# Four of eight normalised tiles of y move from ScalarE to GpSimd in four more batches

## The reference

```python
x = L0_attn_x                                            # (8, 1024, 128)
x = _layernorm(x + _L0_attn_ref(x, wq, wk, wv, wo), axis=-1)
x = _layernorm(x + _L0_ffn_ref(x, w1, b1, w2, b2), axis=-1)

# _layernorm: (x - mean) / sqrt(var + 1e-5), no gain, no bias
# attention: q, k, v = x @ w; rope(q), rope(k); causal softmax(q k^T / 128) @ v @ wo
# ffn: gelu(x @ (alpha1 * sign(w1)).T + b1) @ (alpha2 * sign(w2)).T + b2
```

## Time and profile before

| | |
|---|---|
| median of 3 runs | 279.47 us (278.9 to 280.8) |
| the profiled execution, its own time | 278.4 us |
| its span, first to last instruction | 276.6 us |
| PE busy | 260.7 us, 94% of the span |
| DVE busy | 230.6 us, 83% |
| ACT busy | 224.7 us, 81% |
| POOL busy | 167.2 us, 60% |
| mean granted clock of PE | 0.983 |

### The profile page before, as it was taken

The page is one execution under the profiler, slowest core; times in us unless marked ns, Lnnn a source line. Parts: engine busy times, 40 slices in busy tenths (PEclk is TensorE's granted clock), DMA queues, the critical chain, the costliest instruction groups (busy, mean ns, idle before and its releaser), DMA issues.

```text
span 276.6 us, 5169 instructions
## 1 busy us (share of the span) xinstructions
PE 260.7 (94%) x1478; PEld 209.2 (76%) x1479; DVE 230.6 (83%) x638; ACT 224.7 (81%) x398; POOL 167.2 (60%) x258
## 2 busy tenths in 40 slices
PE   7799999999999999999999999999999999999960
PEld 3588889987688688868879688767885878897630
DVE  2889999999999996999989985999689738537884
ACT  3468964565897989996998999699999699999972
POOL 3033132613625598299912998477829987887772
PEclk9979999999999999999999999999999999999995
DMA  7943486479648936823675309724830720200323
GB/s 180 161 65 71 102 149 108 115 165 192 105 119 186 193 88 153 176 37 85 184 178 122 84 26 246 185 60 126 204 89 5 210 62 0 78 0 2 105 92 110
DMA packets 58012, 31.94 MB, mean 115 GB/s; under 512 B 33408, under 2 KB 54400, under 8 KB 57984
## 3 DMA queue, kind: packets, MB, share of 16 engines
q1 hardware_dynamic: 57024, 30.76, 49.6%
q10 hardware_dynamic: 960, 0.85, 1.2%
HBM read 9.18 MB, written 4.19 MB: 48 GB/s over the span
## 4 chain that ended last, share of the span: by engine, by line
PE 76%; DVE 8%; ACT 5%; DMA 5%; issue 4%; ACTq 1%; POOL 0%; SPq 0%; POOLq 0%; DVEq 0%
PE pair L589 17%; PE bank L606 17%; PE bank L632 5%; PE bank L674 5%; PE bank L620 4%; PE pair L650 4%; PE pair L651 4%; PE bank L682 3%; PE bank L683 3%; DMA out_dram<-res 2%; DMA sin_sb<-in_sin_dram 2%; PE bank L719 2%; PE pair L663 2%; PE bank L639 2%; PE pair L665 2%
## 5 line engine op out<-in xcount | busy, mean ns | idle before, releaser
L391 POOL TENSOR_TENSOR hid_lo<-hid,hid_hi 128x1024 fp32r<-128x1024 f32 x28 | 66.1, 2386 | 21.1 <-ACT hid_hi L1073 21.1
L1002 ACT ACTIVATE prob<-pair,negmax 128x128 f32<-128x128 f32 (+3 forms) x64 | 47.3, 742 | 17.0 <-DVE negmax L1455 15.4
L606 PE MATMUL bank<-probT,xa 128*128 128x512 f32 (+3 forms) x160 | 54.2, 482 | 0.3 <-DVE res L1565 0.3
L1455 DVE CUSTOM_DVE_ANT_0 pair<-pair,mask_row 128x128 f32<-128x128 f32 (+3 forms) x64 | 47.8, 760 | 6.7 <-PE pair L589 6.3
L606 PEld LDWEIGHTS bank<-probT,xa 128*128 128x128 f32 x160 | 29.1, 190 | 20.4 <-issue 15.8
L341 POOL TENSOR_TENSOR xT_lo<-xT,xT_hi 128x512 fp32r<-128x512 f32 x14 | 18.0, 1285 | 40.8 <-ACT xT_hi L1032 40.8
L1465 DVE STREAM_TRANSPOSE turned<-prob 128x128 f32<-128x128 f32 (+7 forms) x56 | 39.5, 723 | 0.5 <-ACT prob L1002 0.5
L589 PE MATMUL pair<-qkT_hi 128*128 128x512 f32 (+3 forms) x96 | 36.5, 380 | 1.4 <-ACT prob L1002 0.6
L589 PE MATMUL pair<-qkT_hi,qkT_lo 128*128 128x512 f32 (+3 forms) x96 | 33.1, 345 | 0.0
L589 PE MATMUL pair<-qkT_lo,qkT_hi 128*128 128x512 f32 (+3 forms) x96 | 33.1, 345 | 0.0
L1066 ACT ACTIVATE hid<-pair,b_sb,alpha 128x1024 f32<-128x1024 f32 x28 | 32.9, 1208 | 0.1
(11 more groups left out here) (116 smaller groups left out, 649.6 us busy)
## 6 DMA issues: line engine op xcount, KB each, us to landing
probT<-turned SPq DMA_DIRECT2D x96, 116.0 KB, 2.3
probT<-turned SPq DMA_DIRECT2D x128, 52.0 KB, 2.0
xq<-in_L_attn_x_dram SPq DMA_DIRECT2D x28, 128.0 KB, 3.9
xa<-in_L_attn_x_dram SPq DMA_DIRECT2D x7, 512.0 KB, 5.1
out_dram<-res SPq DMA_DIRECT2D x7, 512.0 KB, 3.4
hid<-in_L_ffn_w_dram SPq DMA_DIRECT2D x2, 256.0 KB, 3.1
out_dram<-res SPq DMA_DIRECT2D x2, 256.0 KB, 2.3
xa<-in_L_attn_x_dram SPq DMA_DIRECT2D x1, 256.0 KB, 3.6
```

The source lines that it names most:

```text
L391: pool.tensor_tensor(hid_lo[:, j, :], hid[:, j, :], hid_hi[:, j, :].bitcast(F32), ALU.subtract).then_inc(s_hid_lo[j], 1)
L606: ins = pe.matmul(bank_of["px", g, c][:, 0:n * P], xa[c % 2][:, j, :], probT[g][:, :, TG * j:TG * j + n, :].rearrange("p n m i -> p m n i" ...
L1002: act.activation(prob[r % 3][:, 0:(r + 1) * P], pair_of["score", r, c][:, slice(*columns(r))], ACT.Exp, scale=-1.0, bias=negmax[:, r:r + 1 ...
L1455: dve.tensor_tensor_reduce(mine, mine, mask_row[:, T - (r + 1) * P:T], -1.0, -MASKED, ALU.add, ALU.min, negmax[:, r:r + 1]).then_inc(s_max ...
```

## The change

Four calls `second_norm(4, c)` to `second_norm(7, c)` are taken from ACT's list for c = 1, 2, 3 and 4, and written in POOL's list right behind `second_factors(c)`. `SHARED` becomes batches 1 to 6. With it ACT raises `s_y` behind tile 3 in these batches, and `store(c)` also waits for POOL. The lists of PE, DVE and SP stay as they are. Sixteen instructions change engines; none is added or removed. The last hunk of the diff is ACT's list in batch 3; in batches 1, 2 and 4 the four calls stood apart in it and go in the same way. POOL's first call of a group waits for the last factor (`s_ln2`), which POOL itself wrote.

```diff
-    SHARED = (LAST - 2, LAST - 1)
+    SHARED = tuple(range(1, LAST))
...
             second_factors(1)
+            second_norm(4, 1)
+            second_norm(5, 1)
+            second_norm(6, 1)
+            second_norm(7, 1)
             first_factors(1, B - 4)
...
             second_factors(2)
+            second_norm(4, 2)
...
             first_factors(0, B - 3)
...
             second_factors(3)
+            second_norm(4, 3)
...
             first_factors(0, B - 2)
             first_factors(1, B - 2)
             hidden_low(0, B - 3)
...
             second_factors(B - 4)
+            second_norm(4, B - 4)
...
             first_rstd(0, B - 1)
...
             row_copy(7, B - 1)
-            second_norm(4, 3)
-            second_norm(5, 3)
-            second_norm(6, 3)
-            second_norm(7, 3)
             gelu(0, B - 2)
```

More of the change, by code:

```diff
@@ L449, in _ @@
             second_factors(2)
+            second_norm(4, 2)
+            second_norm(5, 2)
+            second_norm(6, 2)
+            second_norm(7, 2)
             first_factors(0, B - 3)
@@ L457, in _ @@
             second_factors(3)
+            second_norm(4, 3)
+            second_norm(5, 3)
+            second_norm(6, 3)
+            second_norm(7, 3)
             first_factors(0, B - 2)
@@ L464, in _ @@
             second_factors(B - 4)
+            second_norm(4, B - 4)
+            second_norm(5, B - 4)
+            second_norm(6, B - 4)
+            second_norm(7, B - 4)
             first_rstd(0, B - 1)
@@ L1306, in _ @@
             second_norm(3, 1)
-            second_norm(4, 1)
             exponentials(5, B - 2)
-            second_norm(5, 1)
-            second_norm(6, 1)
             exponentials(6, B - 2)
-            second_norm(7, 1)
             exponentials(7, B - 2)
@@ L1333, in _ @@
             hidden_high(0, B - 4)
-            second_norm(4, 2)
-            second_norm(5, 2)
             hidden_high(1, B - 4)
@@ L1338, in _ @@
             exponentials(2, B - 1)
-            second_norm(6, 2)
             exponentials(3, B - 1)
@@ L1342, in _ @@
             hidden_high(3, B - 4)
-            second_norm(7, 2)
             exponentials(5, B - 1)
@@ L1390, in _ @@
             second_norm(3, B - 4)
-            second_norm(4, B - 4)
-            second_norm(5, B - 4)
             gelu_half(0, 0, B - 1)
-            second_norm(6, B - 4)
             gelu_half(0, 1, B - 1)
@@ L1397, in _ @@
             gelu_half(0, 3, B - 1)
-            second_norm(7, B - 4)
             y_half(0, B - 2)
```

## The result

| | before | changed |
|---|---|---|
| median of 4 runs | 279.19 us (278.42 to 280.8) | 289.69 us (288.88 to 291.82) |
| ratio | | 1.041, 95% interval 1.035 to 1.048 |
| profiled execution, span | 276.6 us | 287.7 us |
| PE busy | 260.7 us | 263.8 us |
| DVE busy | 230.6 us | 243.9 us |

Slower was forecast, with 5.5 us. It is 10.5 us in the medians and 11.1 us in the two profiled spans. The time lies above the forecast's range, which ended at 286.5 us.

The account below looks back on a forecast made before the run. PE was taken to bound the kernel. Terms -0.1 (ACT), 0 (batch 2), 4.2 (batch 3), 1.2 (clock) and 0.2 (batch 4) gave +5.5 us on 278.4, so 283.9, forecast as 284.4 us; own range 282 to 286.5, 8-in-10 range from 278.9.

Parts of the forecast that it names:

- relief of ACT is worth 0.1 us: Sixteen norms leaving ACT free 6.7 us there, but gain only 0.1 us, at most 0.6, since PE is busy.
- the list of signs: What the profile would show on each engine; for ACT, busy down by 8 us and waits for DVE and PE up.
- A shift of 1.87 us a group: On POOL, each group of four norms delays what stands behind it by 1.87 us, until POOL's next wait.
- Batch 2 costs nothing, though `first_norm(4, 5)` waits: Near 195 us, first_norm(4, 5) waits some 0.9 us for POOL's later factors; taken as 0, could be 0.4 us.
- Batch 3: norm 0 held by `hidden_low(0, 5)`, norms 4 and 5 one behind each following one, 6 and 7 free: DVE's eight first_norm(t, 6), near 228 us, meet POOL's later hidden_low; up(0, 6) on PE starts 4.2 us late.
- the clock: PE's clock falls to the lower level after its stand near 232 us: 1.2 us, between 0 and 1.7.
- DVE keeps the port: Rival, 19%: after norm 3 of batch 6, norms 4 to 7 follow without a gap while POOL waits; 279.5 us median.
- norms 5 to 7 go together: Rival, 12%: in batch 6 these norms all go ahead of hidden_low(2, 5); +2.1 us, 280.5 to 281.5 us.
- That costs 0.2 us, between 0 and 1.5: Batch 4's group delays first_rstd(0, 7), so first_norm(·, 7) meets hidden_low(0, 6); turn_x1(0, 7) stands behind 52 PE matmuls.

Follow-up runs that it names:

- batches 1 and 2 alone: Only the four-norm groups of batches 1 and 2 moved to POOL, against the kernel before: 279.6 us, ratio 1.001.
- the kernels that have this hole alone: Kernel before with only batch 3's group moved to POOL (283.9 us, 1.016), or with four extra norms on POOL behind second_factors(3) (283.9 us, 1.018).
- batch 4 alone: Only batch 4's four norms moved to POOL, against the kernel before: 285.5 us, ratio 1.023.
- the kernel with batch 4's factor first: Only batch 4's group moved to POOL, with first_rstd(0, 7) ahead of its four norms, against the kernel before: 277.5 us, ratio 0.997.
- batch 3's kernel: Only batch 3's four norms moved to POOL, against the kernel before: 283.9 us, ratio 1.016.
- load on POOL alone: Kernel before plus four POOL norms on a table no longer read, behind second_factors(3); ACT and stores unchanged: 283.9 us, ratio 1.018.

## Why the prediction was right and wrong

- *PE bounds it, relief of ACT is worth 0.1 us.* Right as far as the runs tell: 0, give or take 1.2 us, by the run that leaves the norms out. ACT's busy time fell by 5.2 us; the working had 6.7 and the list of signs 8, both too much.
- *A shift of 1.87 us a group.* Right: from L363's end at 219.43 to L323 at 221.28 it is 1.85, where L323 had started 0.04 us before that end.
- *Batch 2 costs nothing, though `first_norm(4, 5)` waits.* Right: the wait in the profile is 0.8 us, and the run with batches 1 and 2 alone is level.
- *Batch 3: norm 0 held by `hidden_low(0, 5)`, norms 4 and 5 one behind each following one, 6 and 7 free.* Right in each step. PE stood 3.05 us where 3.3 were forecast. With the clock the place was to cost 5.4 us and cost 5.0. The two terms by themselves, from the kernels that have this hole alone: 4.0 us for the norms (4.2 forecast), and 0.9 for the clock (1.2 forecast) in the execution where it fell; in the other it did not fall.
- *DVE keeps the port*, and *norms 5 to 7 go together*: refuted by the 4.69 us of the pair at 229.72.
- *"That costs 0.2 us, between 0 and 1.5"*, the term of batch 4: this is the step that failed. It was 5.5 us, and 1.1 more behind it at the lower clock. The mechanism was named, its size was not: the prediction doesn't count how many of the four `first_norm(·, 7)` are held, and lets PE's 52 matmuls cover them. The kernel before had the count in its rows, though not in those that I read out. `first_rstd(0, 7)` ended at 242.40 and POOL then waited for ACT until 243.35; with 1.87 us more it ends at 244.27, ACT's part is ready, and the wait in which the norms started is gone. All four are held, one behind each `hidden_low`, four times 2.35 us: to 253.7, where PE's 52 matmuls end at 248.75. The run with batch 4 alone is this case (norms from 243.98 to 253.27) and costs 6.6 us.
- In the changed kernel the first hole comes on top. `second_factors(4)` also waits for `statistics2(1, 4)` on DVE, which stands behind the held norms: POOL waits 1.72 us for it, to 241.96. It makes the place later, and the kernel with batch 4 alone shows that it isn't needed for the second hole. Of the 9.3 us of norms the 52 matmuls, done at 253.2, hid 4.7; the other 4.6, the 0.6 of `residual2(1, 6)` and 0.15 until PE starts are PE's wait.
- *The sum.* The profiled spans differ by 11.1: 5.0 for batch 3, 5.5 and 1.1 for batch 4, less the 0.5 by which this execution was ahead before. Forecast were 5.4 and 0.2.
- The range failed with that term. It doesn't quite come out of its own terms either: 284.4 without the clock's 1.2 is 283.2 and not 282, and with 1.7 of clock and 1.5 in batch 4 it is 286.2 and not 286.5. Either upper end lies under the 289.7 us measured.

## What to carry to other kernels

When work moves onto GpSimd, look up which of VectorE's instructions can't run beside it, and in which gaps of GpSimd they run now; a gap of 1.8 us that shrinks by 1.1 us let three of seven waiting norms through, and two of the rest were held 2.3 us each. The worst place is a short result that VectorE waits for with a series of long GpSimd instructions right behind it: put a gap or something short there, or a form of the VectorE instruction that doesn't exclude GpSimd. And before you let a reader's other work cover such a place, count the held instructions: one for each of the long ones that follow without a gap.

## What the runs showed of the hardware that was not expected

- The exclusion depends on POOL's instruction. Beside L335 on 128x4, from 200.47 to 201.51 in the kernel before, two `first_norm` took 0.60 us together from 200.78, their full pace. Beside POOL's own 128x128 norms (the kernel with batch 4's factor first, above) only the first of four was held, by 0.15 us, the others kept their pace, and POOL's took up to 521 ns instead of 448 in the median. The Trainium skill ("SBUF — State Buffer", "Who interferes with whom") has one instruction block the other fully; the rows show that only for the `tensor_tensor` over 512 or 1024 columns, where each held norm ends 0.08 us behind it.
- In the series of `hidden_low` that these profiles show, exactly one waiting norm gets in at each boundary (two norms in 4.69 us, four in 9.30 and in 9.29), and POOL gets in between two norms of a series (at 229.66, with norm 4 from 229.72). The engines take turns, which costs the one with the short instructions most.
- PE's clock came down behind both holes of the changed kernel: the eight transposes of 1.04 us took 1.91, and behind the second hole 1.1 us were lost. It doesn't always: behind the same stand of 3.05 us it stayed at 1.00 in batch 3's kernel and fell to 0.50 in the one with load on POOL alone. What decides it stays open.

```profile
200.78 0.60 DVE L1497 TENSOR_SCALAR x<-res,ln 128x128 f32<-128x128 f32 x2
```

The line above is from the timeline of DVE in the kernel before, at the first of these points.
